# Expert stage of a two-layer kernel: TensorE's groups for blocks i, i-2, i-4, and a shorter preloaded residual

## What is computed

```
x = x + attn(layernorm(x))          # r*wkv scan over time, then relu(k)^2 @ Wval, gated
xn = layernorm(x)
gates = sigmoid(xn @ expert_sel.T);  sel_val, sel_idx = top_k(gates, 4)
scores = relu(xn @ keys[e]) * gate   # [256] -> [128], for the 4 chosen experts e
out = x + sum over e of scores @ values[e]   # [128] -> [256]
```

## Time and profile before

| | us |
|---|---|
| timed runs, median of 3 | 1458.73 (1451.87 to 1459.62) |
| span of the profiled execution | 1618.1 |
| mix stage and plan in that span | 0 to about 915 |
| expert stage | about 915 to 1488 |
| combine stage | about 1488 to 1618 |

### The profile page before, as it was taken

One profiled execution on the slowest core, in us unless ns is written; L12 is line 12 of the kernel. 1 busy time (PEld: TensorE's weight loads), 2 busy tenths in 40 slices (PEclk: granted clock), 3 DMA queues, 4 the chain that ended last, 5 costly groups with the idle time before them and its releaser, 6 DMA issues. The chain is left out here.

```text
span 1618.1 us, 28319 instructions
## 1 busy us (share of the span) xinstructions
PE 1184.4 (73%) x7399; PEld 1058.3 (65%) x7400; DVE 1096.5 (68%) x2519; ACT 678.8 (42%) x1265; POOL 889.3 (55%) x967
## 2 busy tenths in 40 slices
PE   6799999999999999999881266766776766773000
PEld 5688887888878887788771266666766666673000
DVE  4889898888988889888847444444544444443987
ACT  2555565445654456444443143443443443442000
POOL 1634676666766677667657455555555555554000
PEclk9899999999999999999985588798788788886555
DMA  5000121111111121121163754445444444434998
GB/s 184 14 27 13 68 70 60 66 53 69 65 59 65 46 78 59 61 70 60 54 274 143 249 151 137 140 137 149 133 146 144 133 143 142 141 113 158 390 390 321
DMA packets 101917, 201.25 MB, mean 124 GB/s; under 512 B 16983, under 2 KB 49901, under 8 KB 100464
## 3 DMA queue, kind: packets, MB, share of 16 engines
q1 hardware_dynamic: 63216, 120.34, 23.6%
q0 software_dynamic: 27648, 67.70, 11.5%
q10 hardware_dynamic: 11008, 12.65, 2.2%
HBM read 105.28 MB, written 103.71 MB: 129 GB/s over the span
## 5 line engine op out<-in xcount | busy, mean ns | idle before, releaser
L1359 POOL DMA_INDIRECT expert_rows<-y,dest x320 | 320.4, 1001 | 257.1 <-issue 224.9
L1124 POOL DMA_INDIRECT lists<-rows,slot x256 | 276.5, 1080 | 73.3 <-issue 70.4
L1269 PE MATMUL ps<-xt_hi,keys 128*128 128x256 f32 x640 | 180.0, 341 | 114.0 <-issue 110.1
L1336 DVE TENSOR_TENSOR xt_lo<-ps,xt_hi 128x512 fp32r<-128x512 f32 x160 | 110.5, 690 | 186.0 <-ACT xt_hi L1296 107.6
L1269 PEld LDWEIGHTS ps<-xt_hi,keys 128*128 128x128 f32 x640 | 131.4, 226 | 130.7 <-issue 129.5
L1308 ACT ACTIVATE y<-ps 128x512 f32<-128x512 f32 x160 | 96.1, 601 | 130.2 <-PE ps L1284 113.2
L535 PE MATMUL ps<-wv_hi,k_hi 128*128 128x256 f32 x512 | 149.6, 292 | 0.0
L537 PE MATMUL ps<-wv_lo,k_hi 128*128 128x256 f32 x512 | 147.8, 289 | 0.9 <-issue 0.9
L539 PE MATMUL ps<-wv_hi,k_lo 128*128 128x256 f32 x512 | 147.6, 288 | 0.3 <-issue 0.3
L1296 ACT ACTIVATE xt_hi<-ps 128x512 fp32r<-128x512 f32 x160 | 96.6, 604 | 122.0 <-PE ps L1256 101.9
L1282 PE MATMUL ps<-experts_w,h_hi 128*128 x320 | 108.4, 339 | 47.6 <-DVE h_lo L1343 36.7
(11 more groups left out here) (201 smaller groups left out, 3544.4 us busy)
## 6 DMA issues: line engine op xcount, KB each, us to landing
xr<-lists SPq DMA_DIRECT2D x160, 260.0 KB
ye<-expert_rows SPq DMA_DIRECT2D x32, 1024.0 KB, 8.1
x_sb<-in_x SPq DMA_DIRECT2D x16, 512.0 KB, 3.8
residual<-xp SPq DMA_DIRECT2D x16, 512.0 KB, 4.9
experts_raw<-in_expert_in SPq DMA_DIRECT2D x8, 1024.0 KB, 15.1
lists<-zeros SPq DMA_DIRECT2D x25, 260.0 KB, 10.8
expert_rows<-y,dest POOLq DMA_INDIRECT x320
resid<-residual SPq DMA_DIRECT2D x20, 256.0 KB, 5.4
```

Of the source, the lines that this page charges most:

```text
L1124: pool.indirect_dma_start(lists, bass.IndirectOffsetOnAxis(ap=slot[:, q, n:n + 1], axis=0), rows[:, q, n // TOPK, :], None).then_inc(scatt ...
L1269: mm = pe.matmul(ps[:, H + q, 0:BLOCK], keys[:, (r - 1) % SLOTS, half, k * DE:(k + 1) * DE], m[:, q, k, :], start=n == 0, stop=n == 3 * KD ...
L1336: dve.tensor_tensor(xt_lo[:, q].rearrange("p k b -> p (k b)"), ps[:, XT + q, :], xt_hi[:, q].rearrange("p k b -> p (k b)").bitcast(F32), A ...
L1359: pool.indirect_dma_start(expert_rows, bass.IndirectOffsetOnAxis(ap=dest[:, r, s:s + 1], axis=0), y[:, r, s, :], None, bounds_check=OUT_RO ...
```

## The change

In the expert stage, TensorE's step i now does transposes of block i, keys of block i-2 (`H_LAG`) and values of block i-4 (`Y_LAG`). ScalarE and VectorE follow with the same lags. `xt_hi`, `xt_lo`, `h_hi`, `h_lo` and the PSUM bank of the transposes have four homes (`SLOTS`); the banks of keys and values stay at two. The waits for free buffers are moved to match. The register load of the expert's number moves behind the keys. `HEAD` goes from 24 to 8 groups, so one turn of four steps of the combine stage finds its residual in SBUF. The instructions are otherwise the same in kind and number.

```
-HEAD = 24
+HEAD = 8
...
     SLOTS = RING // 2
+    H_LAG, Y_LAG = 2, 4
+    HBANKS, YBANKS = 2, 2
...
-    xt_hi, xt_lo = (sb(f"xt_{h}", [P, 2, KD, BLOCK], F32R) for h in ("hi", "lo"))
-    h_hi, h_lo = (sb(f"h_{h}", [P, 2, BLOCK], F32R) for h in ("hi", "lo"))
+    xt_hi, xt_lo = (sb(f"xt_{h}", [P, SLOTS, KD, BLOCK], F32R) for h in ("hi", "lo"))
+    h_hi, h_lo = (sb(f"h_{h}", [P, SLOTS, BLOCK], F32R) for h in ("hi", "lo"))
...
-    XT, H, Y = 0, 2, 4
+    XT, H, Y = 0, SLOTS, SLOTS + HBANKS
...
+    def enters(i):
+        return not isinstance(i, int) or i < NBLOCKS
+    def lagging(i, lag):
+        return not isinstance(i, int) or lag <= i < NBLOCKS + lag
...
         def _(pe):
-                    after(pe, x_ready, i - 1)
+                    after(pe, x_ready, i - SLOTS + 1)
...
-                if not isinstance(i, int) or i >= 2:
-                    e = pe.value_load(plan_expert[0:1, bass.ds(i - 2, 1)], min_val=0, max_val=E - 1)
-                q = (r - 1) % 2
-                if not isinstance(i, int) or 1 <= i <= NBLOCKS:
-                    pe.wait_ge(keys_ready, i)
-                    pe.wait_ge(x_ready, i)
-                    after(pe, h_ready, i - 2)
+                if lagging(i, H_LAG):
+                    b, q = i - H_LAG, (r - H_LAG) % SLOTS
+                    pe.wait_ge(keys_ready, b + 1)
+                    pe.wait_ge(x_ready, b + 1)
+                    after(pe, h_ready, b - HBANKS + 1)
...
-                q = (r - 2) % 2
-                if not isinstance(i, int) or i >= 2:
-                    pe.wait_ge(h_ready, i - 1)
-                    after(pe, ycopy_ready, i - 3)
+                if lagging(i, Y_LAG):
+                    b, q = i - Y_LAG, (r - Y_LAG) % SLOTS
+                    e = pe.value_load(plan_expert[0:1, bass.ds(b, 1)], min_val=0, max_val=E - 1)
+                    pe.wait_ge(h_ready, b + 1)
+                    after(pe, ycopy_ready, b - YBANKS + 1)
...
-            loop(pe, step, drain=2)
+            loop(pe, step, drain=Y_LAG)
...
         def _(act):
                     act.wait_ge(xt_done, i + 1)
-                    after(act, h_done, i - 1)
+                    after(act, h_done, i - SLOTS + 1)
...
-                    act.wait_ge(h_done, i)
-                    after(act, y_done, i - 2)
+                    act.wait_ge(h_done, b + 1)
+                    after(act, y_done, b - SLOTS + 1)
...
-                    act.wait_ge(y_done, i - 1)
-                    after(act, sent[b], 16 * SUB * (ring - 1 if r >= 2 else ring - 2) + 16 * SUB)
+                    act.wait_ge(y_done, b + 1)
+                    after(act, sent[q], 16 * SUB * (ring if r >= Y_LAG else ring - 1))
...
         def _(dve):
-                    dve.wait_ge(hhi_ready, i)
+                    dve.wait_ge(hhi_ready, b + 1)
...
-            loop(dve, step, drain=1)
+            loop(dve, step, drain=H_LAG)
...
     HEAD_RINGS = HEAD // GROUPS // DEPTH
-            with eng.Fori(1, HEAD_RINGS) as ring:
-                for r in range(DEPTH):
-                    step(DEPTH * ring + r, r, ring, True)
```

More of the change, by code:

```diff
@@ L1250, in step @@
             def step(i, r, ring):
-                if not isinstance(i, int) or i < NBLOCKS:
+                if enters(i):
                     pe.wait_ge(rows_loaded[r % SLOTS], 16 * (2 * ring + r // SLOTS + 1))
-                    after(pe, x_ready, i - 1)
+                    after(pe, x_ready, i - SLOTS + 1)
                     for k in range(KD):
                         for s in range(SUB):
-                            mm = pe.transpose(ps[:, XT + r % 2, k * BLOCK + s * P:k * BLOCK + (s + 1) * P],
+                            mm = pe.transpose(ps[:, XT + r % SLOTS, k * BLOCK + s * P:k * BLOCK + (s + 1) * P],
                                               xr[:, r % SLOTS, s, k * P:(k + 1) * P], ident)
                     mm.then_inc(xt_done, 1)
-                if not isinstance(i, int) or i >= 2:
-                    e = pe.value_load(plan_expert[0:1, bass.ds(i - 2, 1)], min_val=0, max_val=E - 1)
-                q = (r - 1) % 2
-                if not isinstance(i, int) or 1 <= i <= NBLOCKS:
-                    pe.wait_ge(keys_ready, i)
-                    pe.wait_ge(x_ready, i)
-                    after(pe, h_ready, i - 2)
+                if lagging(i, H_LAG):
[3 more added lines that the diff above has]
+                    after(pe, h_ready, b - HBANKS + 1)
                     n = 0
@@ L1268, in step @@
                         for half, m in ((0, xt_hi), (0, xt_lo), (1, xt_hi)):
-                            mm = pe.matmul(ps[:, H + q, 0:BLOCK],
-                                           keys[:, (r - 1) % SLOTS, half, k * DE:(k + 1) * DE],
+                            mm = pe.matmul(ps[:, H + q % HBANKS, 0:BLOCK],
+                                           keys[:, q, half, k * DE:(k + 1) * DE],
                                            m[:, q, k, :], start=n == 0, stop=n == 3 * KD - 1)
@@ L1273, in step @@
                     mm.then_inc(h_done, 1)
-                q = (r - 2) % 2
-                if not isinstance(i, int) or i >= 2:
-                    pe.wait_ge(h_ready, i - 1)
-                    after(pe, ycopy_ready, i - 3)
+                if lagging(i, Y_LAG):
[3 more added lines that the diff above has]
+                    after(pe, ycopy_ready, b - YBANKS + 1)
                     v_hi, v_lo = (w[:, h, bass.ds(e, 1), KD * DE:].rearrange("p a w -> p (a w)") for h in (0, 1))
                     for s in range(SUB):
-                        cols = ps[:, Y + q, s * D:(s + 1) * D]
+                        cols = ps[:, Y + q % YBANKS, s * D:(s + 1) * D]
                         c = slice(s * P, (s + 1) * P)
@@ L1291, in step @@
             def step(i, r, ring):
-                q = r % 2
-                if not isinstance(i, int) or i < NBLOCKS:
+                if enters(i):
+                    q = r % SLOTS
                     act.wait_ge(xt_done, i + 1)
-                    after(act, h_done, i - 1)
+                    after(act, h_done, i - SLOTS + 1)
                     act.activation(xt_hi[:, q].rearrange("p k b -> p (k b)"), ps[:, XT + q, :],
                                    ACT.Copy).then_inc(xhi_ready, 1)
-                q = (r - 1) % 2
-                if not isinstance(i, int) or 1 <= i <= NBLOCKS:
-                    act.wait_ge(h_done, i)
-                    after(act, y_done, i - 2)
[L1302 to L1305, removed]
-                    act.wait_ge(y_done, i - 1)
-                    after(act, sent[b], 16 * SUB * (ring - 1 if r >= 2 else ring - 2) + 16 * SUB)
-                    act.activation(y[:, b].rearrange("p s d -> p (s d)"), ps[:, Y + q, :],
+                if lagging(i, H_LAG):
+                    b, q = i - H_LAG, (r - H_LAG) % SLOTS
+                    act.wait_ge(h_done, b + 1)
+                    after(act, y_done, b - SLOTS + 1)
+                    act.activation(h_hi[:, q, :], ps[:, H + q % HBANKS, 0:BLOCK], ACT.Relu).then_inc(hhi_ready, 1)
+                if lagging(i, Y_LAG):
+                    b, q = i - Y_LAG, (r - Y_LAG) % RING
+                    act.wait_ge(y_done, b + 1)
+                    after(act, sent[q], 16 * SUB * (ring if r >= Y_LAG else ring - 1))
+                    act.activation(y[:, q].rearrange("p s d -> p (s d)"), ps[:, Y + q % YBANKS, :],
                                    ACT.Copy).then_inc(ycopy_ready, 1)
-            loop(act, step, drain=2)
+            loop(act, step, drain=Y_LAG)
         @block.vector
@@ L1320, in step @@
             def step(i, r, ring):
-                q, qh = r % 2, (r - 1) % 2
-                a_block = not isinstance(i, int) or i < NBLOCKS
-                if a_block:
+                if enters(i):
+                    q = r % SLOTS
                     if r == 0:
@@ L1326, in step @@
                     after(dve, h_done, i - SLOTS + 1)
-                    dve.tensor_copy(keys[:, r % SLOTS], w[:, :, bass.ds(expert[r], 1), 0:KD * DE].rearrange(
+                    dve.tensor_copy(keys[:, q], w[:, :, bass.ds(expert[r], 1), 0:KD * DE].rearrange(
                         "p h a w -> p (h a) w").bitcast(F32)).then_inc(keys_ready, 1)
@@ L1332, in step @@
                     after(dve, dest_ready, i)
-                    dve.tensor_scalar(mark[:], xr[:, r % SLOTS, :, D:ROW], plan_mark[:, bass.ds(i, 1)], None,
+                    dve.tensor_scalar(mark[:], xr[:, q, :, D:ROW], plan_mark[:, bass.ds(i, 1)], None,
                                       ALU.subtract).then_inc(mark_ready, 1)
@@ L1340, in step @@
                         load_expert(i + 1, r + 1)
-                if not isinstance(i, int) or 1 <= i <= NBLOCKS:
-                    dve.wait_ge(hhi_ready, i)
-                    dve.scalar_tensor_tensor(h_lo[:, qh, :], ps[:, H + qh, 0:BLOCK], 0.0,
-                                             h_hi[:, qh, :].bitcast(F32), ALU.max, ALU.subtract
+                if lagging(i, H_LAG):
```

(8 more changed lines are left out.)

## The result

Side by side, 20 runs each, the changed kernel takes 1458.84 us in the median (1457.17 to 1469.71) and the kernel before 1454.95 (1450.38 to 1459.62). The ratio is 1.0041, 95% interval 1.0027 to 1.0055: 3.9 us by the medians, 6.0 by the ratio, where 9.9 were forecast. On another occasion it was 1457.33 against 1453.04, ratio 1.0037 (1.0021 to 1.0054). So the change makes the kernel slower there, by about 0.4%, some 40 to 60% of what was forecast. The absolute time, 1458.84 where 1469 was forecast, is off by 9.8 us; 3.8 of them are the base, since the median of 3 runs that the forecast started from, 1458.73, fell to 1454.95 with 20.

The account below looks back on a forecast made before the run. The prediction took POOL's 320 scatters, 412.8 us, to bound the expert stage in timed runs. It added 2.5 us for the later start and 7.4 for HEAD to 1458.7, giving 1468.6, 1469 us (+0.7%), range 1446 to 1479.

Parts of the forecast that it names:

- the rule on trace records: Expert stage: the trace-record block holds producers back when its pipeline fills, so gaps would be absent when nothing is recorded.
- 1471.7: Whole kernel: profiled span of 1618.1 us with all 146.4 us of POOL's gaps out, 13.0 above the timed median.
- Part 1: Expert stage: longer lags of keys and values give each hand-over a step more; worth 0 in timed runs, POOL bound.
- Rival 1: Expert stage: late hand-overs partly in timed runs too, gaps up to about 40 us; 1441 with 28 removed; chance 0.23.
- the "half" of 146.4: Expert stage, profiled execution only: the lag recovers half of POOL's 146.4 us of gaps, giving about 1555 us.
- Part 2: Expert stage's start: extra transposes and keys before the first values make POOL start later, +2.5 us, ends 1.0 and 4.5.
- the low end: Expert stage's start: lowest cost given for POOL's later start, 1.0 us.
- Part 6: Last stage: HEAD 24 to 8 makes eight more steps load their own residual, +7.4 us, ends +4.7 and +9.0.
- The low end, 4.7: Last stage: loaded steps at the unloaded stretch's 398 GB/s instead of 365, 3.78 us each, +4.7 us.
- the high end: Last stage: 1.57 MB a step at the loaded stretch's 365 GB/s, 4.31 us each, +9.0 us.
- rival 2: Whole kernel: no difference, POOL-bound with both costs at their low ends, 1458.7 + 1.0 + 4.7 = 1464 us; chance 0.21.
- parts 3 to 5: Expert stage: extra drain steps, register load moved behind keys, and moved waits each cost 0.

## Why the prediction was right and wrong

**What bounds the kernel** was read rightly for the runs it was about: POOL, 1.29 us a scatter. The rule that the timed scatters take 412.8 us and little more holds for the changed kernel (415.3 and 414.1 on two occasions). For the kernel before on such a chip it is argued from a sum, and not seen. The sentence that the late hand-overs are "mostly of the recorded execution" was wrong, and so was the use of the rule on trace records that stood behind it: on the 1617 kind they are in the timed runs too. That the number survived this is luck: the timed runs of the forecast and of the result were both of the 1455 kind. The 13 us by which 1471.7 lay above the median are explained as well. The two kinds also differ before the expert stage: its first transposes start at 918.25 us in the earlier trace rows and at 898.08 in the changed kernel's profile, 20.2 us earlier, with the same instructions up to there. Taken off the 1058.9 us outside the scatters, this leaves 1038.7; a time of 1454.95 has a span of about 1453, so the scatters of the kernel before would take about 414 us on this kind. That is an estimate from profiles of different occasions, good to a few us.

**Part 1** (the lag worth 0 with POOL bound) agrees with that estimate on the 1455 kind. **Rival 1** is what happened on the other kind, where the gaps are in the timed runs; but its price is 18 us, not the "half" of 146.4 that the text gave the profile. The profiles came out at 1602.0 and 1616.2, not about 1555: the lag took back 20 us of gaps, and part 1's picture of a fixed wait of 2.3 us that a step more covers does not fit the bursts.

**Part 2** was put at +2.5. The start of the stage in the changed kernel:

```profile
898.08 1.11 PE L1267 MATMUL ps<-consts,xr 128*128 128x128 f32 x4 [32.48 <-DMA xr<-lists]
...
905.79 0.60 ACT L1317 ACTIVATE y<-ps 128x512 f32<-128x512 f32 x1 [0.77 <-PE ps L1294]
...
907.21 1.00 POOL L1367 DMA_INDIRECT expert_rows<-y,dest  x1 [19.78 <-DVE dest L1357]
```

POOL starts 9.1 us after the first transposes, where the earlier trace rows have 7.8: +1.3, near the low end. But the earlier trace rows are among the lowest: in all eleven profiles with the old lags and homes it is 7.8 to 9.1 us, 8.4 in the mean, and in the four of the changed kernel 9.0 to 10.0, 9.3 in the mean. So the term is about +1.0, with the 1617 kind in both means. The assumption of a low clock was half right: the third group of transposes, which now stands before the first keys, still takes some 1.06 us (eight matmuls in 2.13 for the second and third), the fourth and fifth 0.60.

**Part 6** was put at +7.4 and measured 4.6, and this is the step that failed, with part 2 as the smaller one. The mechanism, eight more steps that load their own residual, was right; the size was not. The mean of 4.12 us for a loaded step came from one profiled execution that had slow ones: counted the same way, the five later profiles of the kernel before have 3.91, 3.93, 3.93, 4.01 and 4.18 us. It also counted the two steps right after the switch, 5.5 and 4.4 us, which are paid wherever the switch stands; without them it is 4.02, and the term 6.6. And with 28 loaded steps in place of 20 a step takes less, 3.86 to 3.96 us in the five profiles of `HEAD = 8` alone, so the eight steps added less than eight means. In the changed kernel:

```profile
1331.80:1344.60 12.80, 0.00 (x0) 0.00 (x0) 12.74 (x32) 0.00 (x0) 0.00 (x0) 0.50 1.00 383
1345.30:1455.10 109.80, 0.00 (x0) 0.00 (x0) 91.16 (x224) 0.00 (x0) 0.00 (x0) 0.50 1.01 388
```

That is 3.20 and 3.92 us a step, 5.8 us for eight by the difference, where the timed pairs have 4.6. The low end, 4.7, has the right size by luck: it assumed a loaded step of 3.78 us, which no profile shows, and its working does not fit that of the high end, since 1.57 MB at 398 GB/s is 3.95 us, or +6.1. The figure of the Trainium skill ("Perfetto Trace Analysis", Roofline), 435 GB/s, would have given 3.4; the measured 4.6 lies between it and my term, the highest rate in a stretch of some 40 us being 408.

The two terms together, 4.6 + 1.0 = 5.6 us, meet the 6.0 and 5.4 us of the two ratios (3.9 and 4.3 by the medians), with the reservation that 4.6 is from chips of the other kind. The last stage at least looks the same on both: from the first addition to the start of the last it takes 122.6, 122.1 and 122.5 us in the three profiles of the 1455 kind and 122.1 to 124.8 in the five of `HEAD = 8` alone. All this is nearest to **rival 2** (both costs low, 1464 from a base of 1458.7, +5.7).

Nothing speaks against **parts 3 to 5**. From the last scatter's start to the first addition it is 9.4 us in both kernels (1322.5 to 1331.9, 1484.2 to 1493.6), so the longer drain costs nothing. The register load behind keys costs nothing where the engine runs freely: the transposes of 907.46 and 909.33 us are 1.87 us apart, where the earlier trace rows have 1.86.

```profile
907.46 0.60 PE L1267 MATMUL ps<-consts,xr 128*128 128x128 f32 x4
...
909.33 0.60 PE L1267 MATMUL ps<-consts,xr 128*128 128x128 f32 x4
```

## What to carry to other kernels

When a profiled execution and the timed median differ by more than a few per cent, first run the unchanged kernel again and look at its span and chip; the difference may be between chips, and a cause found in the profile then holds only for one kind. Price a step moved across a switch by the steady steps on both sides, leave out those next to the switch, and take the mean over more than one profile. A start or a stage that a change moves by 1 us can't be read from one pair of profiles if it varies by as much without the change. Here the longer lag was worth something only where the engine behind the others was starved, and part of its price, the memory taken from a preload, was measured there too: 4.6 us by `HEAD = 8` alone.

## What the runs showed of the hardware

The same kernel takes 1453 us on one chip (and 1455 beside the changed kernel in the first comparison, whose chip is not on record) and 1617 to 1635 us on six others, with nearly the same busy time on VectorE, ScalarE and POOL. TensorE is busy 1184 us against 1141 in the two first profiles, at a lower granted clock: 0.83 in the scatters' stretch, of which it is busy 70%, against 0.96 and 84%.

On the second kind TensorE's completions in the expert stage are signalled in bursts: in the profile shown above 171 of 455 come less than 0.1 us after another, though the groups end at least 0.43 us apart; in the mix stage it is 10 of some 440 on both kinds, and ScalarE there starts 0.04 us (median) after the end of the TensorE group that it waited for, on both kinds too. A TensorE that merely worked slowly would not finish groups so close together, which speaks for the signalling and against TensorE's own work as the place of the lateness; it does not prove it, since the ends of matmuls are modelled and no run changes only this. Why these chips (or occasions) do so, why in this stage alone, and what sets the spacing of the bursts stays open.
